# A one-core attention and expert kernel: its hand-written order of steps re-arranged, TensorE's dummy matmuls at the start changed, and 137 short ones added in the score part

## The reference, cut to what matters

```python
x = L0_attn_x                                  # 4 x 512 x 128, float32
xn = layernorm(x)
x = x + attn(xn, ...) + ffn(xn, ...)
# attn: chunked attention, 16 heads of width 8, chunks of 16 tokens, once on the sequence and once on
#       every third token; both outputs summed, then one linear layer
# ffn:  h = xn + mla(rmsnorm(xn));  out = h + moe(rmsnorm(h))
# mla:  q, k, v over a latent of 32, 16 heads of width 8 with rotary halves, causal softmax over 512 keys
# moe:  one shared expert and the best 2 of 7, gate/up/down of 128 x 128, silu
```

## Time and profile before

| | |
|---|---|
| time, three runs | 378.18 us median (376.24 to 379.63) |
| the profiled execution's own time | 371.83 us |
| its span | 369.6 us |
| busy, PE / PEld | 334.2 us (90%) / 206.3 us (56%) |
| busy, DVE / ACT / POOL | 285.0 us (77%) / 222.3 us (60%) / 123.0 us (33%) |
| chain that ended last | PE 60%, DVE 28%, issue 5%, ACT 3%, DMA 3% |

### The profile page before, as it was taken

The page is one execution under the profiler, slowest core; times in us unless marked ns, Lnnn a source line. Parts: engine busy times, 40 slices in busy tenths (PEclk is TensorE's granted clock), DMA queues, the critical chain, the costliest instruction groups (busy, mean ns, idle before and its releaser), DMA issues.

```text
span 369.6 us, 11664 instructions
## 1 busy us (share of the span) xinstructions
PE 334.2 (90%) x4504; PEld 206.3 (56%) x4504; DVE 285.0 (77%) x720; ACT 222.3 (60%) x545; POOL 123.0 (33%) x148
## 2 busy tenths in 40 slices
...
GB/s 200 77 108 173 71 167 62 67 62 42 40 162 46 36 66 51 78 184 25 43 53 50 65 65 34 36 3 172 5 0 0 3 27 2 4 28 2 29 0 28
DMA packets 29141, 21.84 MB, mean 59 GB/s; under 512 B 12312, under 2 KB 26008, under 8 KB 29048
## 3 DMA queue, kind: packets, MB, share of 16 engines
...
q10 hardware_dynamic: 216, 0.20, 0.2%
...
## 4 chain that ended last, share of the span: by engine, by line
PE 60%; DVE 28%; issue 5%; ACT 3%; DMA 3%; SPq 1%; POOL 0%; DVEq 0%; ACTq 0%; POOLq 0%
PE bank_B L1372 13%; DVE neg_max L1012 9%; PE bank_B L1180 8%; PE bank_c L1276 7%; PE bank_A L1378 7%; PE bank_A L1318 3%; PE bank_M L1283 2%; PE bank_B L1166 2%; DVE s_loc L1029 2%; DVE row_max L1026 2%; PE bank_M L1341 2%; PE bank_M L1221 2%; PE bank_c L1192 2%; PE bank_M L1211 1%; PE bank_M L1326 1%
## 5 line engine op out<-in xcount | busy, mean ns | idle before, releaser
L830 ACT ACTIVATE p_mla<-bank_B 128x512 f32<-128x512 f32 (+1 forms) x176 | 92.0, 561 | 54.6 <-PE bank_B L1166 31.0
L1012 DVE TENSOR_REDUCE neg_max<-bank_A 128x1 f32<-128x512 f32 (+3 forms) x176 | 106.9, 636 | 15.8 <-PE bank_A L1166 13.0
L1180 PE MATMUL bank_B<-q_stack,k_stack 54*128 54x512 bf16 (+3 forms) x256 | 62.4, 306 | 12.1 <-DVE neg_max L1012 8.2
L1159 PE MATMUL bank_A<-k_stack,q_stack 52*128 52x512 bf16 (+3 forms) x256 | 63.1, 307 | 3.2 <-DMA q_stack<-parts 2.2
L1372 PE MATMUL bank_B<-xrT,k_diag 128*128 128x512 f32 x128 | 60.9, 597 | 1.1 <-DVE k_diag L1137 1.1
L703 POOL TENSOR_TENSOR x<-x,q_part 128x512 f32<-128x512 f32 x31 | 39.5, 1274 | 58.0 <-ACT q_part L864 41.7
L1276 PE MATMUL bank_c<-p_mla,v_mla 128*32 128x384 f32 (+12 forms) x512 | 47.6, 453 | 0.4 <-ACT p_mla L830 0.4
L1180 PEld LDWEIGHTS bank_B<-q_stack,k_stack 54*128 54x128 bf16 x256 | 19.4, 94 | 49.6 <-issue 23.4
L864 ACT ACTIVATE q_part<-bank_A,expert_w 128x128 f32<-128x128 f32 x108 | 30.8, 369 | 24.6 <-PE bank_A L1378 24.6
L1137 DVE SCALAR_TENSOR_TENSOR k_diag<-k_diag,bank_B 128x512 f32<-128x512 f32 x32 | 22.0, 687 | 29.1 <-ACT k_diag L848 26.7
L1166 PE MATMUL bank_A<-masks 64*128 64x64 bf16 (+2 forms) x352 | 43.9, 204 | 0.0
(11 more groups left out here) (150 smaller groups left out, 550.4 us busy)
## 6 DMA issues: line engine op xcount, KB each, us to landing
...
```

The costliest lines, as they stand in the source:

```text
L830: drained_by(nc.scalar.activation(p_of(n)[:, m:m + len(heads), 0:w], src, ACT.Exp, scale=SCALE), step)
L1012: drained_by(nc.vector.tensor_reduce(neg_max[:, g, m:m + len(heads), i], src, AX.X, ALU.max, negate=True), step)
L1159: return nc.tensor.matmul(bank_of(step)[:, n * w:(n + 1) * w], q_stack[b % 2][rows, h % 8, i * P:(i + 1) * P], k_stack[b % 2][rows, h % 8, ...
L1180: nc.tensor.matmul(bank_of(step)[:, m * w:(m + 1) * w], k_stack[b % 2][rows, h % 8, j * P:(j + 1) * P], q_stack[b % 2][rows, h % 8, j * P: ...
```

## The change

Three things change.

1. `WARM`: 84 dummy products, all at or ahead of S.0.0 (9 ahead of WF, 2 ahead of XT.0.1, 16, 1 and 5 ahead of MA.0.0, MB.0 and MA.0.1, 12 ahead of XT.0.0, 1 and 5 ahead of LK.0 and LQ.0, 12 ahead of MV.0, 11 ahead of LV.0.0, 10 ahead of S.0.0). The ten single ones of S.0.2 to S.0.11 are gone.
2. `FILL`: 137 bfloat16 products of 128 rows and 192 columns at 36 score steps, between one and eight at each. In a pair, TensorE waits for the E step's bank B, issues the dummies into it, and only then waits for the S step's bank A. Ahead of a single S step they go to `bank_c`, ahead of the last E steps to the bank A of the next DOWN. The E step's own first product overwrites them.
3. `ORDER`: the same 408 steps and the same 198 pairs; some 150 steps move, most by one to three pairs.

```diff
-WARM = {("WF",): 6, ("XT", 0, 1): 2, ("MA", 0, 0): 2, ("S", 0, 0): 10, **{("S", 0, n): 1 for n in range(2, 12)}}
+WARM = {("LK", 0): 1, ("LQ", 0): 5, ("LV", 0, 0): 11, ("MA", 0, 0): 16, ("MA", 0, 1): 5, ("MB", 0): 1, ("MV", 0): 12, ("S", 0, 0): 10, ("WF",): 9, ("XT", 0, 0): 12, ("XT", 0, 1): 2}
+FILLS = {
+    1: """
+    E.0.0.0.0 E.0.3.0.2 E.1.1.1.3 E.2.0.1.3 S.0.15
...
+    7: """
+    E.0.0.0.3 E.2.1.2.0 E.3.1.0.3
+    """,
+    8: """
+    E.3.0.1.2
+    """,
+}
+FILL_WIDTH = 192
...
-LR.3.2 *2 SHIFT.3.1 Y.2.3 PT.3.2 LT.3.1 PICK.1.0 PICK.1.1 LS.3.3 YT.2 LO.3.2 PICK.1.2 *2 LR.3.3 PICK.1.3 X1.2
-PV.3.0.0 PT.3.3 *5 LT.3.2 * PV.3.0.1 * SHIFT.3.2 LS.3.4 PV.3.0.2 * PV.3.0.3 *3 Y.3.0 *2 WX LO.3.3 LR.3.4 * PV.3.1.0
...
+SHIFT.3.1 * LR.3.2 Y.2.3 PICK.1.0 * PT.3.2 LT.3.1 PICK.1.1 LS.3.3 YT.2 LO.3.2 * PICK.1.2 X1.2 LR.3.3 PV.3.0.0 *4
+PICK.1.3 PT.3.3 LT.3.2 *2 PV.3.0.1 PV.3.0.2 * PV.3.0.3 *3 SHIFT.3.2 *2 Y.3.0 PV.3.1.0 * LS.3.4 WX LO.3.3 * PV.3.1.1
...
+            def fill(step, to):
+
+                for _ in range(FILL.get(step, 0)):
+                    nc.tensor.matmul(to[:, 0:FILL_WIDTH], masks[:, 0:P], masks[:, 0:FILL_WIDTH], start=True,
+                                     stop=True, skip_group_check=True)
...
-                if step in where and kind != "SHIFT":
-                    wait_free(pe, step)
+                if step in where:
                     bank = bank_of(step)
+                    if kind not in ("S", "E", "SHIFT"):
+                        wait_free(pe, step)
...
                     if step not in waits_for_e:
+                        fill(step, bank_c)
+                        wait_free(pe, step)
...
                     other = beside.get(step)
+                    if other:
+                        wait_free(pe, step)
+                        fill(step, bank)
+                        wait_free(pe, other)
+                    else:
+                        if step in FILL:
+                            wait_free(pe, next_down[step])
+                            fill(step, bank_of(next_down[step]))
+                        wait_free(pe, step)
```

75 lines of the change are left out of this document (48 added, 27 removed).

## The result

The change is slower. In five executions each the median went from 376.24 us (373.46 to 379.63) to 385.72 us (385.65 to 392.22); the ratio is 1.034, with a 95% interval of 1.028 to 1.040. I had forecast +0.9%. Every ratio in this text compares only the executions that the clock disturbed less, here four of the change's five.

What follows compares the result with a forecast made beforehand. TensorE bounds the expert part; in the score part TensorE and VectorE wait on each other, and the clock falls. 8.5 - 0.9 + 1.5 - 4.5 - 1.1 = +3.5 us on 371.8, scaled to 381.7 us; range 374.5 to 388.

Steps and rivals of the forecast that it cites:

- The start: Up to S.0.0: 64 more dummies make the first score product 8.5 us late, bounds 5.5 and 10.5.
- walk: Step-by-step timing of TensorE's start from 3.90 us, putting MA.0.0 at 13.85 and S.0.0 at 34.6 us, four fills included.
- The single dummies: S.0.2 to S.0.11: removing ten dummies pays back 0.9 us, two of 0.42 us in the chain; bounds 0 and -4.4.
- The fills: Score steps: 137 fills last 11.6 us on TensorE, an eighth taken as cost, +1.5 us; bounds 0 and 11.6.
- the fills are served on the path: Slower rival, score part: fills between both bank waits cost half of 11.6 us; sum +7.8, 386 us; chance 0.14.
- the two long waits: TensorE's waits for VectorE's maxima in the score part: 1.00 us at 132.58 and 1.14 us at 241.54.
- The clock: Score part: fills prevent four falls to 1.2 GHz; two thirds of 6.8 us gained, -4.5 us; bounds 0 and 6.8.
- cap of 6.8: Upper bound of the clock gain: 1.7 us of TensorE's time lost in each of four score-part stretches.
- the factor of 1.0171: Median of the runs shown over the profiled execution, 378.18 to 371.83; it scales the forecast 375.3 to 381.7 us.
- The order: Score part: moved steps save half of the 1.14 and 1.00 us waits, -1.1 us; bounds -3 and +2.
- the distance from S.0.0 to the first GU: Sign over the score part: the prediction is wrong if this shrinks by more than 8 us or grows.
- The length from the first GU on: Sign for the expert part, to the end: the same length within 1 us.

## Why the prediction was wrong

**The start: right in mechanism and size, with a bound too narrow.** S.0.0 came at 34.26 us where the clock rose early (walk: 34.6 with 0.35 of fills, so 34.25), MA.0.0 at 13.83 (walk: 13.85). In the change's own profile the clock rose later, and S.0.0 was 12.0 us late, beyond the bound of 10.5. I had let the later rise cost "1.5 to 2 us more", since I counted only the first dummies at 0.47 us; about half of the sixteen ahead of MA.0.0 ran at the lower level too.

**The single dummies: mis-sized, -0.9 for -2.6 to -4.5.** I priced them by the pieces that the chain shows. Ten of 0.42 us, 4.2 in all, on an engine that hands banks to and fro with another were worth between six tenths and the whole of their sum. The late start and this term together are the WARM table's 6.4 us at full clock; I had 7.6.

**The fills: the step that failed.** "I take an eighth of the 11.6 us" came from the waits of 1.00 and 1.14 us. The value was 8.4 us, 0.06 for each fill. The rival "the fills are served on the path" was right in mechanism, and its price of half was still too low. That its 386 us are the measured 385.72 is luck: it had 2.6 us too little for the fills and 3.7 too little for the order, and this was in part made up for by 1.2 us too much at the WARM table, by 1.3 us of the clock's gain that it missed, and by a median of 378.18 us for before where five executions gave 376.24. What misled me: fills stand at 36 places and the two long waits are at two of them. The earlier trace rows should have bounded the hidden part: of its 8.2 us in 19 places only the seven places with fills count, with waits of 4.2 us and fills to go into them of 1.8. That leaves 9.7 us of fills without such a wait, within the uncertainty of the 8.4 measured and far from my 1.5. Besides, a wait for VectorE's maxima is not all free time when VectorE itself waits for TensorE's next scores.

**The clock: right on the mean.** The falls vanished from the profile with the fills alone, and the mean clock rose by 0.019 in the change, worth 5.8 us; I had 4.5 and a cap of 6.8 from one trace. I had put all of it down to the fills, but the new order alone raised the mean clock by 0.013. The mean clock of before's executions, 0.967, is below the 0.978 of the one profiled, so that there was more to win than the cap said. This is also about half of the 6.35 us behind the factor of 1.0171: at 3.0 us per 0.01 it makes some 3 us, and the profiled execution was one of the fastest besides.

**The order: wrong in sign, small.** -1.1 for +2.6 at full clock (ratio 1.003). I priced the two waits that the moves soften and called SyncE's queue harmless after looking at batch 1 only; whether the cost lies there, the experiments do not show.

**The signs.** Of the signs that I named one said that I was wrong: the distance from S.0.0 to the first GU grew, by 10.1 us, where my terms behind the start come to -5.0. The length from the first GU on shrank by 1.3 us, a little more than the 1 us I allowed, as it does in the profile of the new order alone (94.7 us for 96.0).

Together, at full clock: 16.9 us longer, less 5.8 for the clock, 11.1 in the mean spans. My +3.5 lacked 6.9 at the fills, 3.7 at the order, and had 1.2 too much at the WARM table and 1.3 too little at the clock; 3.5 + 6.9 + 3.7 - 1.2 - 1.3 = 11.6, and the 0.5 us beyond is what the three parts alone have over the whole.
